# Expert stage of a sequence kernel: TensorE's groups at blocks i, i-2 and i-4, and plan entries read in batches

## The reference

```python
x = x + _L0_attn_ref(_layernorm(x), ...)
x = x + _L0_ffn_ref(_layernorm(x), expert_sel, keys, values)
# _L0_ffn_ref, over N = 8192 tokens, 32 experts of 128, top 4:
gates = jax.nn.sigmoid(xt @ expert_sel.T)
sel_val, sel_idx = jax.lax.top_k(gates, 4)
gate_full = zeros.at[arange(N)[:, None], sel_idx].set(sel_val)
scores = relu(einsum('nd,edf->nef', xt, keys)) * gate_full[:, :, None]
out = einsum('nef,efv->nv', scores, values)
```

## Time and profile before

| | |
|---|---|
| median of 3 runs | 1602.18 us (1601.1 to 1603.06) |
| the profiled execution | 1615.93 us, its span 1614.1 us |
| mean granted TensorE clock | 0.865 of full |
| busy: TensorE, VectorE, ScalarE, GpSimd | 1161.0, 1042.1, 737.4, 864.9 us |
| DMA | 201.25 MB, mean 125 GB/s |

### The profile page before, as it was taken

The page is one execution under the profiler, slowest core; times in us unless marked ns, Lnnn a source line. Parts: engine busy times, 40 slices in busy tenths (PEclk is TensorE's granted clock), DMA queues, the critical chain, the costliest instruction groups (busy, mean ns, idle before and its releaser), DMA issues. The chain is left out here.

```text
span 1614.1 us, 28314 instructions
## 1 busy us (share of the span) xinstructions
PE 1161.0 (72%) x7399; PEld 1046.6 (65%) x7400; DVE 1042.1 (65%) x2424; ACT 737.4 (46%) x1393; POOL 864.9 (54%) x935
## 2 busy tenths in 40 slices
PE   6799999999999999999751476766776677673000
PEld 5688888888887888888651466666666666663000
DVE  4878888787887787887547344444444444443877
ACT  3655667555676556676342244333434343432000
POOL 0524676766676766675636355555555555553000
PEclk9899999999999999999875688888888878887555
DMA  5000221221221121221535644444444444435999
GB/s 184 14 27 10 71 77 63 73 70 42 72 75 62 69 69 46 72 73 54 198 128 217 191 141 139 140 138 140 134 144 140 136 139 143 136 105 177 381 365 333
DMA packets 101917, 201.25 MB, mean 125 GB/s; under 512 B 16983, under 2 KB 49901, under 8 KB 100464
## 3 DMA queue, kind: packets, MB, share of 16 engines
q1 hardware_dynamic: 63216, 120.34, 23.9%
q0 software_dynamic: 27648, 67.70, 11.5%
q10 hardware_dynamic: 11008, 12.65, 2.2%
HBM read 105.28 MB, written 103.71 MB: 129 GB/s over the span
## 5 line engine op out<-in xcount | busy, mean ns | idle before, releaser
L1359 POOL DMA_INDIRECT expert_rows<-y,dest x320 | 318.1, 994 | 267.5 <-issue 238.0
L1127 POOL DMA_INDIRECT lists<-rows,slot x256 | 301.1, 1176 | 74.5 <-issue 70.8
L1269 PE MATMUL ps<-xt_hi,keys 128*128 128x256 f32 x640 | 184.2, 347 | 138.1 <-issue 120.9
L1336 DVE TENSOR_TENSOR xt_lo<-ps,xt_hi 128x512 fp32r<-128x512 f32 x160 | 110.3, 690 | 210.8 <-ACT xt_hi L1296 126.8
L1269 PEld LDWEIGHTS ps<-xt_hi,keys 128*128 128x128 f32 x640 | 134.6, 231 | 153.6 <-issue 152.8
L1296 ACT ACTIVATE xt_hi<-ps 128x512 fp32r<-128x512 f32 x160 | 96.7, 604 | 140.5 <-PE ps L1256 95.6
L859 DVE TENSOR_TENSOR k_lo<-ksq,k_hi 128x512 fp32r<-128x512 f32 x128 | 100.6, 813 | 85.9 <-ACT k_hi L652 65.4
L1308 ACT ACTIVATE y<-ps 128x512 f32<-128x512 f32 x160 | 96.0, 600 | 131.0 <-PE ps L1284 84.6
L535 PE MATMUL ps<-wv_hi,k_hi 128*128 128x256 f32 x512 | 146.0, 285 | 0.0
L537 PE MATMUL ps<-wv_lo,k_hi 128*128 128x256 f32 x512 | 144.8, 283 | 0.0
L539 PE MATMUL ps<-wv_hi,k_lo 128*128 128x256 f32 x512 | 144.8, 283 | 0.0
(11 more groups left out here) (201 smaller groups left out, 3461.2 us busy)
## 6 DMA issues: line engine op xcount, KB each, us to landing
xr<-lists SPq DMA_DIRECT2D x160, 260.0 KB
ye<-expert_rows SPq DMA_DIRECT2D x32, 1024.0 KB, 8.1
x_sb<-in_x SPq DMA_DIRECT2D x16, 512.0 KB
residual<-xp SPq DMA_DIRECT2D x16, 512.0 KB, 4.6
experts_raw<-in_expert_in SPq DMA_DIRECT2D x8, 1024.0 KB, 22.5
lists<-zeros SPq DMA_DIRECT2D x25, 260.0 KB, 10.9
expert_rows<-y,dest POOLq DMA_INDIRECT x320
resid<-residual SPq DMA_DIRECT2D x20, 256.0 KB, 5.6
```

The lines of the kernel that those rows point to most:

```text
L1127: pool.indirect_dma_start(lists, bass.IndirectOffsetOnAxis(ap=slot[:, q, n:n + 1], axis=0), rows[:, q, n // TOPK, :], None).then_inc(scatt ...
L1269: mm = pe.matmul(ps[:, H + q, 0:BLOCK], keys[:, (r - 1) % SLOTS, half, k * DE:(k + 1) * DE], m[:, q, k, :], start=n == 0, stop=n == 3 * KD ...
L1336: dve.tensor_tensor(xt_lo[:, q].rearrange("p k b -> p (k b)"), ps[:, XT + q, :], xt_hi[:, q].rearrange("p k b -> p (k b)").bitcast(F32), A ...
L1359: pool.indirect_dma_start(expert_rows, bass.IndirectOffsetOnAxis(ap=dest[:, r, s:s + 1], axis=0), y[:, r, s, :], None, bounds_check=OUT_RO ...
```

## The change

In the expert stage:

- TensorE's step i now does the transposes of block i, the key products of block i-2 (`H_LAG`) and the value products of block i-4 (`Y_LAG`). The transposed block, `xt_hi`, `xt_lo`, `h_hi` and `h_lo` have four slots (`SLOTS`) instead of two; of the eight PSUM banks four hold transposes, two hidden blocks, two results. The waits that guard a slot move accordingly.
- ScalarE and VectorE follow with the same lags. The drain has four steps instead of two.
- SyncE reads eight entries of `plan_row` at the start of a ring of 8, VectorE eight of `plan_expert`, TensorE four of `plan_expert` before the value products of every fourth block, each with one load for all (`values_of`), where each read one entry a step.
- HEAD goes from 24 to 8: the residual of 8 x 128 rows is loaded ahead, so that the first 4 steps of the combine use it, not the first 12.

The splitting of the weights in the mix is as it was.

```diff
-HEAD = 24
+HEAD = 8
...
+    H_LAG, Y_LAG = 2, 4
+    HBANKS, YBANKS = 2, 2
...
-    xt_hi, xt_lo = (sb(f"xt_{h}", [P, 2, KD, BLOCK], F32R) for h in ("hi", "lo"))
-    h_hi, h_lo = (sb(f"h_{h}", [P, 2, BLOCK], F32R) for h in ("hi", "lo"))
+    xt_hi, xt_lo = (sb(f"xt_{h}", [P, SLOTS, KD, BLOCK], F32R) for h in ("hi", "lo"))
+    h_hi, h_lo = (sb(f"h_{h}", [P, SLOTS, BLOCK], F32R) for h in ("hi", "lo"))
...
-    XT, H, Y = 0, 2, 4
+    XT, H, Y = 0, SLOTS, SLOTS + HBANKS
...
+    def values_of(eng, table, first, n, top):
+        _, values = nc.values_load_multi_w_load_instructions(
+            table[0:1, bass.ds(first, n)], engines=(eng.engine,), min_val=0, max_val=top)
+        return values
...
 # SyncE
+                if r == 0:
+                    rows[:] = values_of(sp, plan_row, i, RING, LIST_ROWS - BLOCK)
                 after(sp, xt_done, i - SLOTS + 1)
                 after(sp, mark_ready, i - SLOTS + 1)
-                row = sp.value_load(plan_row[0:1, bass.ds(i, 1)], min_val=0, max_val=LIST_ROWS - BLOCK)
...
 # TensorE
                     pe.wait_ge(rows_loaded[r % SLOTS], 16 * (2 * ring + r // SLOTS + 1))
-                    after(pe, x_ready, i - 1)
+                    after(pe, x_ready, i - SLOTS + 1)
...
-                if not isinstance(i, int) or i >= 2:
-                    e = pe.value_load(plan_expert[0:1, bass.ds(i - 2, 1)], min_val=0, max_val=E - 1)
-                q = (r - 1) % 2
-                if not isinstance(i, int) or 1 <= i <= NBLOCKS:
-                    pe.wait_ge(keys_ready, i)
-                    pe.wait_ge(x_ready, i)
-                    after(pe, h_ready, i - 2)
+                if lagging(i, H_LAG):
+                    b, q = i - H_LAG, (r - H_LAG) % SLOTS
+                    pe.wait_ge(keys_ready, b + 1)
+                    pe.wait_ge(x_ready, b + 1)
+                    after(pe, h_ready, b - HBANKS + 1)
...
-                q = (r - 2) % 2
-                if not isinstance(i, int) or i >= 2:
-                    pe.wait_ge(h_ready, i - 1)
-                    after(pe, ycopy_ready, i - 3)
+                if lagging(i, Y_LAG):
+                    b, q = i - Y_LAG, (r - Y_LAG) % SLOTS
+                    if q == 0:
+                        expert[:] = values_of(pe, plan_expert, b, SLOTS, E - 1)
+                    pe.wait_ge(h_ready, b + 1)
+                    after(pe, ycopy_ready, b - YBANKS + 1)
...
 # ScalarE
                     act.wait_ge(xt_done, i + 1)
-                    after(act, h_done, i - 1)
+                    after(act, h_done, i - SLOTS + 1)
...
 # VectorE
                     if r == 0:
-                        load_expert(i, r)
+                        expert[:] = values_of(dve, plan_expert, i, RING, E - 1)
...
-                    if r < RING - 1:
-                        load_expert(i + 1, r + 1)
-                if not isinstance(i, int) or 1 <= i <= NBLOCKS:
-                    dve.wait_ge(hhi_ready, i)
+                if lagging(i, H_LAG):
+                    b, q = i - H_LAG, (r - H_LAG) % SLOTS
+                    dve.wait_ge(hhi_ready, b + 1)
...
 # combine
-            with eng.Fori(1, HEAD_RINGS) as ring:
-                for r in range(DEPTH):
-                    step(DEPTH * ring + r, r, ring, True)
```

More of the change, by code:

```diff
@@ L1216, in loop, with enters, lagging @@
             step(i, i % RING, i // RING)
+    def values_of(eng, table, first, n, top):
+        _, values = nc.values_load_multi_w_load_instructions(
+            table[0:1, bass.ds(first, n)], engines=(eng.engine,), min_val=0, max_val=top)
+        return values
+    def enters(i):
+        return not isinstance(i, int) or i < NBLOCKS
+    def lagging(i, lag):
+        return not isinstance(i, int) or lag <= i < NBLOCKS + lag
     def settled_on(eng, s, n, also=None):
@@ L1268, in step @@
                         for half, m in ((0, xt_hi), (0, xt_lo), (1, xt_hi)):
-                            mm = pe.matmul(ps[:, H + q, 0:BLOCK],
-                                           keys[:, (r - 1) % SLOTS, half, k * DE:(k + 1) * DE],
+                            mm = pe.matmul(ps[:, H + q % HBANKS, 0:BLOCK],
+                                           keys[:, q, half, k * DE:(k + 1) * DE],
                                            m[:, q, k, :], start=n == 0, stop=n == 3 * KD - 1)
@@ L1285, in step @@
                     mm.then_inc(y_done, 1)
-            loop(pe, step, drain=2)
+            loop(pe, step, drain=Y_LAG)
         @block.scalar
@@ L1299, in step @@
-                if not isinstance(i, int) or 1 <= i <= NBLOCKS:
[L1300 to L1308, removed]
+                if lagging(i, H_LAG):
+                    b, q = i - H_LAG, (r - H_LAG) % SLOTS
+                    act.wait_ge(h_done, b + 1)
+                    after(act, y_done, b - SLOTS + 1)
+                    act.activation(h_hi[:, q, :], ps[:, H + q % HBANKS, 0:BLOCK], ACT.Relu).then_inc(hhi_ready, 1)
@@ L1309, in step @@
+                if lagging(i, Y_LAG):
+                    b, q = i - Y_LAG, (r - Y_LAG) % RING
+                    act.wait_ge(y_done, b + 1)
+                    after(act, sent[q], 16 * SUB * (ring if r >= Y_LAG else ring - 1))
+                    act.activation(y[:, q].rearrange("p s d -> p (s d)"), ps[:, Y + q % YBANKS, :],
                                    ACT.Copy).then_inc(ycopy_ready, 1)
-            loop(act, step, drain=2)
+            loop(act, step, drain=Y_LAG)
         @block.vector
@@ L1314, in _ @@
         def _(dve):
-            expert = {}
-            def load_expert(i, r):
-                expert[r] = dve.value_load(plan_expert[0:1, bass.ds(i, 1)], min_val=0, max_val=E - 1)
+            expert = [None] * RING
             def step(i, r, ring):
-                q, qh = r % 2, (r - 1) % 2
-                a_block = not isinstance(i, int) or i < NBLOCKS
-                if a_block:
+                if enters(i):
+                    q = r % SLOTS
                     if r == 0:
-                        load_expert(i, r)
+                        expert[:] = values_of(dve, plan_expert, i, RING, E - 1)
@@ L1326, in step @@
                     after(dve, h_done, i - SLOTS + 1)
-                    dve.tensor_copy(keys[:, r % SLOTS], w[:, :, bass.ds(expert[r], 1), 0:KD * DE].rearrange(
+                    dve.tensor_copy(keys[:, q], w[:, :, bass.ds(expert[r], 1), 0:KD * DE].rearrange(
                         "p h a w -> p (h a) w").bitcast(F32)).then_inc(keys_ready, 1)
@@ L1350, in step @@
                                       apply_absolute_value=True).then_inc(dest_ready, 1)
-            loop(dve, step, drain=1)
+            loop(dve, step, drain=H_LAG)
         @block.gpsimd
@@ L1380, in combine_phase @@
     HEAD_RINGS = HEAD // GROUPS // DEPTH
-    assert HEAD % (GROUPS * DEPTH) == 0
+    assert HEAD == GROUPS * DEPTH
     def sum_of(i, r, head):
```

28 lines of the change are left out of this document (15 added, 13 removed).

## The result

The changed kernel takes 1584.88 us (median of 4, 1582.04 to 1587.44) beside 1601.76 of the kernel before (1601.1 to 1603.06): a ratio of 0.9894, interval 0.9877 to 0.9911. It is 17 us faster where 38 were forecast (1564 us); the direction was right, the size less than half. Its profiled execution is 1587.44 us with a span of 1585.6.

A forecast was written before the change was run, and what follows sets the result against it. The prediction took the expert stage as bound by waits in a ring, GpSimd running dry while TensorE's results came late. Terms -58 + 9 + 8 + 3 = -38 took 1602.2 to 1564 us, range 1455 to 1620.

The forecast's parts named there:

- Depth, -58 us: Expert stage: larger lags and four slots give 4.04 blocks a run, 0.36 us less a block over 160 blocks.
- count blocks per run: one more ... and half a block: GpSimd's scatter runs: one block finished ahead plus half from faster refill, 2.54 blocks becoming 4.04.
- hold: Expert stage: TensorE's results reach others late while GpSimd runs back to back, coming free about when its run has drained.
- The tie of the hold to GpSimd: Expert stage: late TensorE results last until GpSimd's scatters drain; inferred from times, no row showing the cause.
- rival 1: Expert stage: GpSimd becomes the bound, kept fed by depth; 1459 us, or 1536 with half the gaps; chance 0.28.
- Loads, +9: Plan entries at ring starts: batched loads cost 9 us where GpSimd is not in a run, ends 0 and 37.
- The lump: VectorE at a ring's start: eight entries' load and checks together, 2.4 to 4.6 us, middle 3.5.
- Head, +8: Combine: eight steps lose their preloaded residual, 1.02 us each, 8 us; by bytes alone 6.
- Start, +3: Expert stage's start: first values at step 4 instead of 2, first batched loads ahead; 3 us, ends 1 and 5.
- GpSimd as the bound: Expert stage: a hold has its own length, depth keeps GpSimd fed; 1459 to 1536 us, chance 0.28.
- Slower: the lumps: Expert stage: depth gives 0, each ring pays its batched loads on VectorE; +48, 1650 us, at measured ends +15 to +59.
- Slower, given 0.20: Whole kernel: the chance that the change makes it slower, beside faster 0.75 and same 0.05.

The follow-up runs named there:

- the version with the head of 16: The changed kernel with every plan entry read by itself and HEAD = 16: 1590.6 us against 1609.1 for the kernel before, ratio 0.9889.
- half of the scatters: The kernel before with one scatter a block in place of two: 1359.6 us, 0.8496 of the kernel before (1601.5).
- plain writes: The kernel before with GpSimd's scatters replaced by one plain SyncE write a block: 1365.1 us against 1601.5; on another chip 1359.7 against 1450.2.
- the pause: The changed kernel with one small GpSimd multiplication behind each block's two scatters, awaited before the next block's: 1655.0 us, 1.032 of the kernel before (1602.9).

## Why the prediction was right and wrong

*Depth, -58 us*: measured 21 (14 to 28). The mechanism held: scatters in runs, fewer gaps, each much as long as before (2.4 to 2.7 us in the mean). The step that failed is "count blocks per run: one more ... and half a block". Depth made 2.4 blocks 2.9 with single loads, half a block more and not one and a half; in after it was 3.2 and 3.0. The prediction counted what the deeper pipeline could finish ahead by its lags and passed over what it quotes itself, two banks each for H and Y, which before had too. With y held in both, TensorE can't start a third, so a hold releases two finished y and one that follows: three blocks, six scatters. The traces bear this out where the wait is for y. In the version with the head of 16, 50 of 53 runs are of 6 scatters, and TensorE stands 118.0 us (45 times) for the y copy and 5.8 for `h_lo`. In after itself it stands longer for the hidden bank (57.8 us against 22.7), and the run is mostly of 6 scatters there too. So a third y bank alone may not be enough; no run has a third bank of either kind, and the cap is argued from the waits, not shown by taking it away. Lags 3 and 6 fit it (no longer runs, the same time), but prove less than they seem to: VectorE's 89.7 us of waits for landed scatters, with GpSimd allowed to lag two blocks instead of four, could cap the runs as well. And after's own runs of 8 (14 of 50, fewer with single loads) go beyond the cap, which stays unexplained.

*The tie of the hold to GpSimd*, inferred from times: right on this kind of chip, and shown (half of the scatters, plain writes, the pause). Its cause inside the chip is not. What it missed is that it belongs to some chips. Of eight chips that the experiments met, four had it (before at 1601 to 1612, as on the chip of the result, which may be one of them), four did not (1449 to 1451). There rival 1's bound, GpSimd without a gap, holds already for the kernel before, and the outcome is the slower one. No row of one trace could have shown that; what makes the chips differ stays open.

*Loads, +9*: on the first kind of chip after stands at 0.9884 with them and at 0.99 without (two chips), -3 us with some 6 of error: nothing, they disappear behind holds that come anyway. Without holds they cost 7 us (3 to 11) together with depth. The lump itself: eight entries load in 598 ns, against 306 for one. The idle before the key copies went from 31.3 to 68.9 us, but the prediction read the first figure wrongly: 15.6 of the 31.3 and 19.5 of the 68.9 are the start of the stage. At each of the other 19 rings it was 0.8 us and is 2.9, where the prediction has 1.65 and 3.5; the growth, 2.0, is the 1.9 that it forecast. In a ring's start at 1108.78 the load and eight checks of 0.275 us make 2.8.

```profile
L1223 PEldq TENSOR_LOAD <-plan_expert x40: 330/334/761, 910.8 to 1428.0; - x40
L1223 DVEq TENSOR_LOAD <-plan_expert x19: 594/598/645, 923.1 to 1406.0; - x19
```

So on VectorE a further entry costs (598 - 306) / 7 = 42 ns, nearer to one transfer than to eight. The price is not even: four entries took TensorE 334 ns, hardly more than one (306), and eight nearly twice that. The 200 ns for each register of the Trainium skill (Runtime: NRT & Kernel Launch, section Instruction fetch mechanics), by which eight would be 1.6 us (an estimate from it), is not what this trace shows (the page has it from loads out of HBM, these tables lie in SBUF); the measured 0.6 decides.

*Head, +8*: the combine grew by 4.1 us in the profiled pair, and the head alone cost 0.38% on the second kind of chip (5.5 us, 3 to 8): the estimate by bytes, 6, was the better one. The 1.02 us of difference for a step was large because the profiled execution of before was slow in the combine (4.21 a step beyond the head; on chip 12 it was 3.96, which makes 6 us of eight steps). After's four steps of the head and the start of the 28 beyond them, which take 4.08 each to 1582.81:

```profile
1454.65 12.75 DVE L1436 SCALAR_TENSOR_TENSOR resid_head<-ye,gates,resid_head 128x256 f32<-128x256 f32 x32 [19.98 <-DMA ye<-expert_rows]
1468.43 3.25 DVE L1436 SCALAR_TENSOR_TENSOR resid<-ye,gates,resid 128x256 f32<-128x256 f32 x8 [1.03 <-DMA resid<-residual]
```

*Start, +3*: 3.5. *Sum*: -21 for depth, its start included, +5 for the head and nothing for the loads are -16; measured -17. So nearly the whole miss is the size of the depth term, 58 forecast and 21 measured; that the loads' 9 fell away made it smaller.

*Rivals.* GpSimd as the bound (1459 to 1536) did not come where results are late: the holds grew with the runs (the longest late result of the count is 3.9 us in before and 5.0 in after), as the prediction's own reading had it. "Slower: the lumps" had half of the mechanism (TensorE stops again in a longer run) and the wrong price; its +15 to +59 are the ends of the lump alone, +26 to +70 with head and start. Slower, given 0.20, is what happened on the chip of the second kind, for another reason.

## What to carry to other kernels

Before pricing a deeper pipeline, find the buffers with the fewest copies on the way to the bound engine: they may cap what can be finished ahead, whatever the lag. A run with still more lag hints at a cap; a run with one more copy of the buffer would show it, and was not made here. Where an engine waits for another's finished work and no wait in the program explains it, ask first whether another chip shows it: here the sign of the change hangs on that, and a version for all chips should be timed on both kinds. A batch of loads is worth checking at the stage's start, where nothing hides it.

## What was not expected of the hardware

The same program takes 1450 us on chips 3, 9, 12 and 15 and 1601 to 1612 on chips 2, 4, 5 and 13, and on one chip it varies by under 1%. On the second set TensorE's results reach ScalarE up to 6.1 us late (the version with the head of 16) while GpSimd issues scatters 0.30 us apart, and arrive on time with 0.8 us or more between them. SyncE's instructions are uneven there too, in the last stretch of the mix where GpSimd's scatters are dense; min/median/max ns, kernel before on the chip of the result, then on chip 12:

```profile
L324 SPq FUSED_REGOPS  x16: 4/37/652, 865.1 to 895.6; - x16
```

```profile
L324 SPq FUSED_REGOPS  x16: 37/37/48, 854.5 to 882.8; - x16
```

A register operation that mostly takes 37 ns takes 652 in one place and 4 in another. What makes it so, the traces do not say. And with a wait for its own small multiplication in between, GpSimd needs 0.86 us from the multiplication's end to the next scatter, against 0.30 from scatter to scatter.
